# Feed-forward of a gated cross-attention block: reciprocals, residuals and statistics of later chunks placed elsewhere in the engines' order, and the second norm applied by ScalarE from chunk 1 on

## The reference

```python
# x, ctx: (16, 128, 256) float32
x = x + tanh(g_xattn) * xattn(layernorm(x), ctx, ctx, gamma)
x = x + tanh(g_ffn) * ffn(layernorm(x), gate_w, up_w, down_w, gate_scale, up_scale, down_scale)

def xattn(q, k, v, gamma):      # 8 heads of 16 rows, 256 queries and keys each
    qk = einsum('bhdq,bhdl->bhql', qh, kh) / sqrt(16)
    return gamma * einsum('bhql,bhdl->bhdq', softmax(qk), vh)

def qmm(x, w, scale):           # weights rounded to fp8 (e4m3), then used as float32
    return einsum('bsi,io->bso', x, w.astype(float8_e4m3fn).astype(float32)) * scale

def ffn(x, ...):                # 256 -> 768 -> 256
    return qmm(silu(qmm(x, gate_w, gate_scale)) * qmm(x, up_w, up_scale), down_w, down_scale)
```

## Time and profile before

| | us |
|---|---|
| median of 3 runs | 263.59 (261.38 to 264.61) |
| profiled execution, its own time | 264.65 |
| its span, first to last instruction | 262.5 |
| TensorE busy in the span | 227.5 |
| VectorE, ScalarE, GpSimd busy | 170.2, 120.3, 135.7 |

### The profile page before, as it was taken

One profiled execution on the slowest core, in us unless ns is written; L12 is line 12 of the kernel. 1 busy time (PEld: TensorE's weight loads), 2 busy tenths in 40 slices (PEclk: granted clock), 3 DMA queues, 4 the chain that ended last, 5 costly groups with the idle time before them and its releaser, 6 DMA issues.

```text
span 262.5 us, 4652 instructions
## 1 busy us (share of the span) xinstructions
PE 227.5 (87%) x1768; PEld 132.9 (51%) x1768; DVE 170.2 (65%) x327; ACT 120.3 (46%) x229; POOL 135.7 (52%) x157
## 2 busy tenths in 40 slices
PE   1799999979979999999998999945957993999982
PEld 0347565644644555655655453422743662576571
DVE  3686868997997797669876306405625645555764
ACT  1014765673573586656865562510522351254340
POOL 6831513796792794836624001151393797575530
PEclk9999999997997999999999977995997999799998
DMA  5996001110130122221132210312200020002022
GB/s 160 309 376 175 4 0 42 41 44 0 47 114 9 45 51 91 66 82 46 39 103 81 69 46 0 93 70 89 80 2 0 0 82 0 2 0 80 2 80 80
DMA packets 19782, 17.74 MB, mean 68 GB/s; under 512 B 4016, under 2 KB 19248, under 8 KB 19760
## 3 DMA queue, kind: packets, MB, share of 16 engines
q1 hardware_dynamic: 19760, 17.44, 21.2%
HBM read 11.02 MB, written 6.42 MB: 66 GB/s over the span
## 4 chain that ended last, share of the span: by engine, by line
PE 60%; DVE 17%; POOL 7%; DMA 6%; issue 4%; SPq 3%; ACT 2%; POOLq 1%; DVEq 0%
PE ps L641 18%; PE ps L684 12%; PE ps L728 11%; DVE neg_max L482 8%; PE ps L654 8%; PE ps L744 5%; PE ps L657 3%; DMA u_scr<-u_sb 3%; DVE nm_parts L494 3%; POOL f_lo L381 2%; DMA gates<-in_L_xattn_gamma 2%; POOL x_sb L337 2%; POOL u_n L334 2%; PE ps L668 1%; PE ps L671 1%
## 5 line engine op out<-in xcount | busy, mean ns | idle before, releaser
L641 PE MATMUL ps<-km,qn 32*128 32x512 f32 x256 | 95.4, 683 | 8.0 <-POOL qn L301 5.8
L482 DVE TENSOR_REDUCE neg_max<-ps 128x2 f32<-128x512 f32 x128 | 81.1, 684 | 24.9 <-PE ps L641 24.6
L415 ACT ACTIVATE p_t<-ps 128x512 f32<-128x512 f32 x128 | 70.8, 599 | 54.8 <-PE ps L657 54.7
L654 PE MATMUL ps<-qm,c_sb 32*128 32x512 f32 x256 | 92.6, 656 | 0.7 <-ACT p_t L415 0.7
L728 PE MATMUL ps<-w_exp,w_gu 128*128 128x512 f16 x192 | 50.2, 410 | 16.0 <-DVE p_t L594 16.0
L641 PEld LDWEIGHTS ps<-km,qn 32*128 32x128 f32 x256 | 37.2, 201 | 26.6 <-DVE neg_max L482 14.1
L381 POOL TENSOR_TENSOR f_lo<-p_t,f_hi 128x512 fp32r<-128x512 f32 x23 | 29.2, 1271 | 38.9 <-ACT f_hi L444 38.9
L657 PE MATMUL ps<-max_t,sel 4*128 4x256 bf16 x256 | 44.5, 272 | 0.0
L294 POOL TENSOR_SCALAR km<-c_sb,mask 128x256 f32<-128x256 f32 x32 | 15.8, 505 | 44.3 <-PE ps L641 42.8
L728 PEld LDWEIGHTS ps<-w_exp,w_gu 128*128 128x128 f16 x192 | 18.2, 103 | 38.5 <-DVE p_t L594 16.0
L654 PEld LDWEIGHTS ps<-qm,c_sb 32*128 32x128 f32 x256 | 34.8, 189 | 2.5 <-issue 1.2
(11 more groups left out here) (66 smaller groups left out, 207.8 us busy)
## 6 DMA issues: line engine op xcount, KB each, us to landing
u_scr<-u_sb SPq DMA_DIRECT2D x32, 128.0 KB
u_n<-u_scr SPq DMA_DIRECT2D x16, 128.0 KB
r_n<-r_scr SPq DMA_DIRECT2D x16, 128.0 KB
out_x<-p_t SPq DMA_DIRECT2D x16, 128.0 KB, 1.8
x_sb<-in_x SPq DMA_DIRECT2D x3, 512.0 KB, 7.9
c_sb<-in_ctx SPq DMA_DIRECT2D x3, 512.0 KB, 8.7
w_all<-in_L_ffn_gate_w SPq DMA_DIRECT2D x1, 768.0 KB, 9.2
w_all<-in_L_ffn_up_w SPq DMA_DIRECT2D x1, 768.0 KB, 9.8
```

The lines of the kernel that those rows point to most:

```text
L415: nc.scalar.activation(p_t[:, b % 2, i, :], ps[:, PS_ST + n % BANKS, :], ACT.Exp, scale=DH ** -0.5).then_inc(exp_ok, 1)
L482: nc.vector.tensor_reduce(neg_max[:, b % 2, at:at + PAR], ps[:, PS_S + n % BANKS, :].rearrange("p (e l) -> p e l", e=PAR), axis=AX.X, op=A ...
L641: nc.tensor.matmul(ps[:, PS_S + n % BANKS, :], qn[rows, b % 2, P * t:P * (t + 1)], km[rows, b % 2].rearrange("p e l -> p (e l)"), start=Tr ...
L654: nc.tensor.matmul(ps[:, bank, :], c_sb[rows, b, P * t:P * (t + 1)], qm[rows, b % 4].rearrange("p e l -> p (e l)"), start=True, stop=False)
```

## The change

- **SyncE**: the reciprocals of chunks 0 to 2 are loaded right behind their save, ahead of `save_u(4c+2)`.
- **VectorE**: `reciprocals` of chunks 0, 1 and 2 stand behind batches 7, 11 and 15 (before: behind 8, behind 12 and its `norm_chunk(0)`, and at the end, which is the same place as behind 15); `reciprocals(3)` behind (0,4) in place of (0,1); `norm_chunk(2)` behind (0,3) in place of (0,5). `norm_chunk(3)` stays behind (1,5).
- **GpSimd**: `attention(2)` before the first `f_lo` in place of behind (0,4); `attention(3)` behind (1,2) in place of (1,4); `rstd_chunk(2)` behind (0,4) in place of (0,5), `rstd_chunk(3)` behind (2,0) in place of (1,5); `result(c-1)` behind (c,4) in place of (c,3). `rstd_chunk` has one operation more, `shift2` = `neg_m2` * `rstd2` (128x4), with a semaphore `sh2_ok`. The norm of chunk 0 stays on GpSimd.
- **ScalarE**: the norm of chunks 1 to 3, as `Identity` with scale `rstd2` and bias `shift2`, behind `f_hi` of tile 1 of the chunk before.

```diff
                 if k == 1 and c > 0:
                     save_reciprocals(c - 1)
-                if k == 2 and c > 0:
                     load_reciprocals(c - 1)
...
             def rstd_chunk(c):
                 pool.wait_ge(v2_ok, c + 1)
-                nc.gpsimd.tensor_tensor(rstd2[:, CH * c:CH * (c + 1)], veps2[:, CH * c:CH * (c + 1)],
-                                        mhalf[:], ALU.pow).then_inc(r2_ok, 1)
-
-            def norm_apply(c):
+                at = slice(CH * c, CH * (c + 1))
+                nc.gpsimd.tensor_tensor(rstd2[:, at], veps2[:, at], mhalf[:], ALU.pow).then_inc(r2_ok, 1)
                 pool.wait_ge(r2_ok, c + 1)
-                if c:
-                    pool.wait_ge(t_ok, c)
-                for q in range(CH):
-                    t = CH * c + q
+                nc.gpsimd.tensor_tensor(shift2[:, at], neg_m2[:, at], rstd2[:, at], ALU.mult).then_inc(sh2_ok, 1)
+
+            def norm_apply_first():
+                for t in range(CH):
+                    q = t
                     nc.gpsimd.tensor_scalar(xn2[:, q, :], x_sb[:, t, :], neg_m2[:, t:t + 1], rstd2[:, t:t + 1],
                                             ALU.add, ALU.mult).then_inc(n2_ok, 1)
...
             rstd_chunk(1)
+            attention(2)
...
-                    if it == 1 and c + 1 < NCH:
-                        norm_apply(c + 1)
-                    if it == 3 and 0 < c < NCH - 1:
+                    if c == 0 and it == 4:
+                        rstd_chunk(2)
+                    if c == 1 and it == 2:
+                        attention(3)
+                    if c == 2 and it == 0:
+                        rstd_chunk(3)
+                    if it == 4 and 0 < c < NCH - 1:
                         result(c - 1)
-                    if c < 2 and it == 4:
-                        attention(c + 2)
-                    if c < 2 and it == 5:
-                        rstd_chunk(c + 2)
...
+            def norm_apply(c):
+                act.wait_ge(sh2_ok, c + 1)
+                act.wait_ge(t_ok, c)
+                for q in range(CH):
+                    t = CH * c + q
+                    nc.scalar.activation(xn2[:, q, :], x_sb[:, t, :], ACT.Identity, bias=shift2[:, t:t + 1],
+                                         scale=rstd2[:, t:t + 1]).then_inc(n2_ok, 1)
...
+                    if it == 2 and c + 1 < NCH:
+                        norm_apply(c + 1)
                     if it == 4 and c + 1 < NCH:
                         chunk_high(c + 1)
...
-                if b == 8:
+                if b in (7, 11, 15):
                     v.wait_ge(coef_ok, 1)
-                    reciprocals(0)
+                    reciprocals((b - 7) // CH)
...
                 if b == 12:
                     norm_chunk(0)
-                    reciprocals(1)
-            reciprocals(2)
...
-                    if c == 0 and it == 1:
+                    if c == 0 and it == 4:
                         reciprocals(3)
...
-                    if it == 5 and c < 2:
+                    if (c, it) in ((0, 3), (1, 5)):
                         norm_chunk(c + 2)
```

More of the change, by code:

```diff
@@ L92, in build @@
         neg_m2 = sb("neg_m2", [P, NB])
+        shift2 = sb("shift2", [P, NB])
         xn2 = sb("xn2", [P, CH, L])
@@ L171, in build @@
         r2_ok = sem("r2_ok")
+        sh2_ok = sem("sh2_ok")
         n2_ok = sem("n2_ok")
@@ L364, in _ @@
                     rstd_chunk(0)
-                    norm_apply(0)
+                    norm_apply_first()
                 if b == 13:
```

## The result

The changed kernel takes 242.75 us (median of 4 runs, 242.27 to 245.78), the kernel before 262.49 in the same comparison; ratio 0.930, 95% interval 0.918 to 0.941. The prediction was 242.5, range 239 to 250. The profiled execution of after took 242.51 us, its span 240.7, where before had 264.65 and 262.5.

The account below looks back on a forecast made before the run. TensorE's gate/up pace was taken to bound the feed-forward, broken by three holes. Gains 8.1 + 12.1 + 0.9 = 21.1 us off the profiled 264.65 gave 243.55; that execution lay 1.06 above the median, hence 242.5, range 239 to 250.

Parts of the forecast that it names:

- What bounds, and the pace: Feed-forward: TensorE bounds it, gate/up every 2.69 us, 17.72 us a chunk without holes; three holes where VectorE waits.
- Hole 1: Chunk 0, VectorE idle 7.91 us at reciprocals(3) for the sums' DMA; moving it behind (0,4) gains 8.1 us.
- Hole 2: Chunk 1, VectorE idle 5.16 us at norm_chunk(2) for GpSimd's x_sb; attention(2) ahead of all f_lo gains 6.2 us.
- Hole 3: Chunk 2, the same wait at norm_chunk(3); attention(3) behind f_lo (1,2) gains 6.2 us less 0.3 charged.
- rival (c): Small waits add up, from GpSimd's full queue, a longer Identity or a locked port: 247 us; chance 0.11.
- Norm on ScalarE: Four Identity operations a chunk behind f_hi of tile 1: 0.59 us from the rows, 0.5 taken each, 2.0 a chunk.
- rival (b): ScalarE's Identity needs other tables than Tanh, 1.28 us a load, two at each norm_apply: 249 us; chance 0.05.
- Attention: Attention batches: moved reciprocals and an earlier attention(1) gain 0.9 us net, bounds 0 and 1.5.
- Rival (a): The r_n loads of chunk 2 come late, GpSimd waits ahead of all f_lo: 7 us lost, 250 us; chance 0.08.
- Rival (d): TensorE's clock falls to 1.2 GHz in unbroken work; slower than before, up to 312 us; chance 0.03.
- (e): The wait only moves elsewhere in VectorE's order, most is given back: 258 to 264 us; chance 0.03.

Follow-up runs that it names:

- e2: Kernel before with only reciprocals 0 to 2 behind batches 7, 11, 15 and the r_n loads right behind the save: 258.62 us against 264.13.
- e6b: Kernel before with only reciprocals(3) moved from behind (0,1) to behind (0,4): 255.43 us against 263.26.
- e5b: Changed kernel with attention(2) back behind f_lo (0,4), norm_chunk(2) and rstd_chunk(2) behind (0,5): 249.88 us, kernel before 263.26.
- e7b: Changed kernel with the two small 128x4 products of norm_chunk made by GpSimd instead of VectorE: 241.19 us, kernel before 263.26.
- e1: Changed kernel with the norm of chunks 1 to 3 back on GpSimd behind f_lo (c,1): 242.73 us, kernel before 264.13.
- e10b: Changed kernel with the small products and the norm of chunks 1 to 3 both on GpSimd: 241.62 us, kernel before 263.49.
- c1b: Changed kernel, unaltered, measured again as yardstick: 241.98 us, kernel before 263.26.
- e3: Changed kernel with the r_n loads back at their old place behind save_u(4c+2): 255.51 us, kernel before 264.13.

## Why the prediction was right, point by point

**The number.** 242.5 against 242.75 is closer than the sum deserves. The sum takes 21.1 us off; the two traces differ by 21.8, the medians of that comparison by 19.7, and the two later ones by 21.3 and 21.1. Which executions were caught decides a microsecond either way.

**What bounds, and the pace.** Three holes with VectorE's wait at the head, and 17.72 us for an unbroken chunk: each unbroken chunk of the runs took 17.62 to 17.79.

**Hole 1.** Predicted 8.1, measured 8.67. I had charged 0.7 us for VectorE coming after TensorE, but `chunk_low(1)` ended at 178.30, just as TensorE came free at 178.36. Counted from the first gate/up, that is the 180.0 of before's scale; my 179.9 took TensorE to run dry at 173.65, where its row gives 173.77 (180.25 less 6.48). `attention(2)` cost `f_lo` 0 nothing, and VectorE's instructions overlap the ones before by 0.05 to 0.1 us (176.34 under the end of 175.67 + 0.75), which I had not counted. The sums were there, as no bracket shows. That the earlier `r_n` loads make the sums come sooner was true (e2) but not needed for this hole (e6b).

**Hole 2.** Predicted 6.2, measured 6.19; put back by e5b it costs 6.0.

**Hole 3.** Predicted 5.9 with 0.3 charged for `fu` (2,0), measured 5.26. The place was right and the size three times too small (0.9), and the reason I gave for it (the queue behind `attention(3)`) was wrong: it was the lock on `norm_chunk(3)`'s products, which I had named as a risk and priced only inside rival (c). Without it (e7b) the queue costs nothing. The Trainium skill, SBUF — State Buffer, "Who interferes with whom", has both halves of it: a VectorE instruction in a two-port mode and a GpSimd instruction block each other for the whole instruction, and one with at most one SBUF input outside these modes doesn't contend. The traces agree with both halves: here 0.17 us became 1.10, and the gate products, which read PSUM and one SBUF tile, kept their 0.68 and 0.75. Which mode the 128x4 products ran in no row shows.

**Norm on ScalarE.** 0.59 us from three rows against 0.591 measured; 2.07 us for four against 2.0. One table load: rival (b) didn't occur. The sum gave the move no gain of its own; by e1 and e10b it has one (1.3 us) only as long as the small products are on VectorE.

**Attention.** Predicted 0.9, measured 1.66 to the first gate/up, of which `weighted(6)` to `weighted(13)` gives 1.4 (58.68 to 57.28): the cast of batch 14 fell from 1.30 to 0.19 us. The other 0.26 is luck and lies before: the first `weighted` came 0.6 us later, and the next six took 0.8 less, which also differs between traces of the changed kernel (54.4 in after, 55.2 in c1b). Behind `weighted(13)` the two traces are alike (15.07 and 15.05), with 3.6 us for `weighted(14)` in both.

**Rival (a)** was priced at 7 us and measured 9.1 in chunk 0 by e3: TensorE dry for 7.1, as priced (`r_n` was there 10.9 us behind the first gate/up, 10.8 in the price), and 2.0 for the work at the lower clock behind the hole, which I had left out. It stayed away because `r_n` came far earlier than my 5.5 us: loads issued until 157.99 were used at 161.33. In e3, with saves of `u` around them, they took 5.7 us. Rival (d) didn't occur: the clock is 1.00 in each window of 5 us from 160 to 235. Nor did (e): no bracket of VectorE at `s_sp` or `x_sb` is left in the feed-forward. Of (c), the locked port came, at 0.9 us, and no gate/up fell to 1.2 GHz.

## What to carry to other kernels

A wait that stands in one engine's order in front of work for others costs them all its length; look at what the engine could do first, and move the one line (e6b: 8.8 us of the 20). After each such move, look at who runs beside the moved instruction: two 128x4 products on VectorE cost 0.6 to 2.1 us because GpSimd was in a long operation. Read parts of a change one at a time before adding them: the loads' place and the reciprocals' each shortened hole 1 (4.8 and 8.8 us), and together they did no more than the second alone (8.7).

## What the runs showed of the hardware that was not expected

The spread of the times (240 to 246 us for one kernel) comes in part from where TensorE's granted clock falls near the end of attention: from `weighted(13)` to the first gate/up it takes 15.05 us in after, 13.48 in c1b and 11.85 in e5b. (The first `weighted` also starts anywhere from 32.9 to 35.2 us, which no run explains.) The same 32 matmuls of `weighted(14)` took 3.6 us in after and 1.9 in e2, and the first gate/up of the new order started anywhere from 157.6 to 162.0 us. Windows of after, then of e2:

```profile
156.00:159.00 3.00, 3.00 (x32) 1.16 (x24) 2.97 (x5) 0.00 (x0) 0.00 (x0) 0.50 0.33 113
```

```profile
156.00:159.00 3.00, 3.00 (x35) 1.27 (x28) 2.97 (x6) 0.51 (x2) 0.00 (x0) 1.00 0.20 59
```

From 150 to 153 us TensorE is shown with 3.00 busy in after and 2.56 in e2, from 147 to 150 with 2.34 and 2.78, so the busy share of the rows doesn't tell which will fall. Nor does the length of a wait alone: behind 1.93 us of idle time the gate/up (2,2) of e3 took 3.51 us, behind 2.23 us that of e1 took 1.90.

A held product catches the gap between two GpSimd operations or misses it: at 200.82 in after the second product got in ahead of an `f_lo` that started at the same hundredth, in e1 and e3 it didn't, for 1.2 us more.

The same loss stands twice in attention, in every trace, untouched by the change. In after:

```profile
76.51 2.03 DVE L505 CAST nm_parts<-neg_max 128x16 bf16<-128x16 f32 x1
```

GpSimd is then in an operation over 128x1536 from 75.08 to 78.51, where the cast ends too; at 56.91 it is the same, with one until 58.89. In most batches this cast takes 0.19 or 0.40 us. What the two cost the whole was not tried.
